# The attention stage of an RWKV-type block on eight cores: the order of its k, v and r projections, and where the Sigmoid stands

## What is computed

```python
xn = _ln(x, ln1_g, ln1_b)
xp = _shift(xn)
k = (xn * mix_k + xp * (1.0 - mix_k)) @ Wk
v = (xn * mix_v + xp * (1.0 - mix_v)) @ Wv
r = jax.nn.sigmoid((xn * mix_r + xp * (1.0 - mix_r)) @ Wr)
# wkv: a = ew * a + exp(k_t) * v_t;  b = ew * b + exp(k_t);  out = a / (b + 1e-8)
wkv = _wkv(k, v, time_decay, time_first)
x = x + r * wkv @ Wo
yn = _ln(x, ln2_g, ln2_b)          # ... then channel mixing and the FFN
```

## Time and profile before

| | |
|---|---|
| Time, median of 3 runs (lowest to highest) | 4658.79 us (4657.66 to 4661.13) |
| Profiled execution: its time, span of core 5 | 4664.68 us, 4663.1 us |
| Spans of the eight cores | 4631.3 to 4663.1 us |
| PE, PEld busy | 3025.4 us (65%), 1208.8 us (26%) |
| DVE busy | 1479.8 us (32%) |
| ACT busy | 1278.9 us (27%) |
| Table loads at line 650 and at line 656 | 64 and 64, 1283 ns each |
| Chain that ended last, by engine | PE 39%, DMA 20%, DVE 20%, ACT 11%, issue 8% |

### The profile page before, as it was taken

How to read it: one execution, slowest core, us unless ns; L and a number is a source line. 1 busy time by engine, 2 the same in 40 slices (tenths; PEclk the granted TensorE clock), 3 DMA queues, 4 the chain that set the end, 5 groups by cost and what they waited for, 6 DMA issues and landing times.

```text
span 4663.1 us, 41167 instructions; the slowest of 8 cores (4631.3 to 4663.1 us)
## 1 busy us (share of the span) xinstructions
PE 3025.4 (65%) x11840; PEld 1208.8 (26%) x11840; DVE 1479.8 (32%) x2843; ACT 1278.9 (27%) x1846; POOL 168.6 (4%) x292
## 2 busy tenths in 40 slices
PE   1112289968468856876486847695587558775867
PEld 0000023223123312332132313331233223321322
DVE  3212323421452144214422253214511552135221
ACT  1132232221421323221432242224313242214221
POOL 2111201200000000000000000000000000000000
PEclk9556566679679977988798968897898779896988
DMA  7565446534223321433132412342243214340323
GB/s 152 159 190 167 150 153 192 178 99 124 71 79 118 111 90 61 129 102 125 52 113 85 130 72 90 88 131 88 75 122 105 97 52 127 99 138 36 115 90 111
DMA packets 260844, 521.09 MB, mean 112 GB/s; under 512 B 26081, under 2 KB 81633, under 8 KB 250386
## 3 DMA queue, kind: packets, MB, share of 16 engines
q1 hardware_dynamic: 178096, 387.52, 26.6%
q0 software_dynamic: 24192, 79.28, 5.3%
q10 hardware_dynamic: 58338, 51.66, 3.9%
HBM read 457.54 MB, written 60.82 MB: 111 GB/s over the span
## 4 chain that ended last, share of the span: by engine, by line
PE 39%; DMA 20%; DVE 20%; ACT 11%; issue 8%; DVEq 1%; POOL 1%; ACTq 1%; SPq 0%; POOLq 0%
PE psO L809 14%; PE psA L841 9%; PE psB L841 8%; DMA fvb<-s_w 3%; DMA fvb<-s_fv 3%; DMA s_w<-stb 2%; DVE bigbf L580 2%; DVE stB_sum L497 2%; DVE sc_bb L571 2%; DMA s_fv<-stb 2%; DVE sc_bb L663 2%; ACT L650 2%; ACT L656 2%; DVE sc_aa L701 1%; PE psT L544 1%
## 5 line engine op out<-in xcount | busy, mean ns | idle before, releaser
L809 PE MATMUL psO<-fvb,bigbf 128*128 128x512 bf16 x4096 | 1078.5, 399 | 217.0 <-DMA fvb<-s_w 68.1
L613 PE MATMUL psO<-bigbf,wsm 128*128 128x512 bf16 x1024 | 341.9, 491 | 531.5 <-ACT bigbf L650 220.8
L809 PEld LDWEIGHTS psO<-fvb,bigbf 128*128 128x128 bf16 x4096 | 393.5, 101 | 841.8 <-issue 461.4
L841 PE MATMUL psB<-TB,fkb 128*128 128x512 bf16 x2048 | 522.4, 401 | 41.1 <-DMA fkb<-s_fk 36.3
L841 PE MATMUL psA<-TB,fkb 128*128 128x512 bf16 x2048 | 514.8, 397 | 21.0 <-DMA fkb<-s_fk 13.4
L867 DVE TENSOR_TENSOR bigbf<-bigbf 128x512 bf16<-128x512 bf16 x256 | 108.4, 425 | 688.0 <-ACT bigbf L863 688.0
L934 DVE SCALAR_TENSOR_TENSOR T<-Q,psO 128x512 f32<-128x512 f32 x64 | 44.0, 688 | 860.4 <-PE psO L927 855.0
L613 PEld LDWEIGHTS psO<-bigbf,wsm 128*128 128x128 bf16 x1024 | 113.7, 116 | 754.0 <-issue 694.9
L506 ACT ACTIVATE zt<-T,stB_nm 128x1024 bf16<-128x1024 f32 x64 | 73.5, 1148 | 851.7 <-DVE stB_m L503 849.2
L841 PEld LDWEIGHTS psB<-TB,fkb 128*128 128x128 bf16 x2048 | 206.7, 102 | 325.5 <-issue 125.1
L544 PE MATMUL psT<-ident_sb,ztm 128*128 128x128 bf16 x512 | 69.6, 292 | 332.6 <-DVE ztm L523 194.4
(11 more groups left out here) (138 smaller groups left out, 3094.5 us busy)
## 6 DMA issues: line engine op xcount, KB each, us to landing
fkb<-s_fk SPq DMA_DIRECT2D x256, 256.0 KB, 2.8
fvb<-s_fv SPq DMA_DIRECT2D x256, 256.0 KB, 2.8
fkb<-s_w SPq DMA_DIRECT2D x256, 256.0 KB, 2.8
fvb<-s_w SPq DMA_DIRECT2D x256, 256.0 KB, 2.8
stq<-L_ffn_fc_q ACTq DMA_DIRECT2D x128, 256.0 KB, 4.4
x<-xcore SPq DMA_DIRECT2D x8, 2048.0 KB, 10.1
wsm<-s_wk SPq DMA_DIRECT2D x16, 1024.0 KB, 7.0
wsm<-s_wr SPq DMA_DIRECT2D x16, 1024.0 KB, 8.9
```

Of the source, the lines that this page charges most:

```text
L613: E("tensor", lambda e, mo=mo, k=k, ps=ps, wt=wt: e.matmul(ps[:], wt[:, 1024 * (k % 4) + 128 * mo:1024 * (k % 4) + 128 * (mo + 1)], bigbf[ ...
L809: E("tensor", lambda e, mm=mm, j=j, mpar=mpar, sl=sl: e.matmul(psO[j][:], bigbf[:, 512 * mm + 128 * j:512 * mm + 128 * (j + 1)], fvb[:, 10 ...
L841: E("tensor", lambda e, m=m, k=k, ps=ps, par=par: e.matmul(ps[:], fkb[:, 1024 * par + 128 * k:1024 * par + 128 * (k + 1)], TB[:, 512 * k:5 ...
```

## The change

The v loop and the scan for b become one loop, and the r loop moves behind it.

- After the k loop comes a loop over `mo` with the v projection and, on VectorE in this order, `ekv`, `sa`, `ca`, `sb`, `cb`, `wk`; on ScalarE `ew`, `lb`, `eb`. One decay tile serves both scans, and `ew2` is gone. `eb` writes back into `sc_bb`, and `wk` multiplies `sc_aa` with it into `T2`.
- A last loop has the r projection. Sigmoid goes into a new tile `rsg` (128 x 512, one buffer) and `gt` multiplies it with `T2`. Sigmoid and `gt` of block `mo` are recorded behind the matmuls of block `mo` + 1.
- The weight buffers hold other matrices: Wv's halves are in `wsm2` and `wsm0`, Wr's in `wsm1` and `wsm2`, Wo's in `wsm0` and `wsm1`.
- In chunk 0 the cast jobs come in the order Wk, Wv, Wr, and of the 52 pairs 10 stand ahead of `stage_mix_vr`, 24 in the k loop, 8 in the v loop (both casts on ScalarE), and the last 10 in the first five passes of the r loop. None is left for the Wo loop.

The diff, without the removed v loop (old lines 687 to 721), the call that records the last Sigmoid, and the two added `pump_pair()` calls ahead of chunk 0:

```diff
@@ -234,6 +234,7 @@
+        rsg = T("rsg", [128, 512], BF16)
@@ -357,8 +358,8 @@
-        for wname, whbm, scr in [("s_wk", Wk, s_wk), ("s_wr", Wr, s_wr),
-                                 ("s_wv", Wv, s_wv), ("s_wo", Wo, s_wo),
+        for wname, whbm, scr in [("s_wk", Wk, s_wk), ("s_wv", Wv, s_wv),
+                                 ("s_wr", Wr, s_wr), ("s_wo", Wo, s_wo),
                                  ("s_wfr", Wfr, s_wfr)]:
@@ -624,8 +625,8 @@
-            E("q_sync", lambda e: e.dma_start(out=wsm[2][:], in_=s_wr[0]),
-              reads=["s_wr@0", "s_wr@1"], writes=["wsm2"], tag=f"{hh}_ldr0")
+            E("q_sync", lambda e: e.dma_start(out=wsm[2][:], in_=s_wv[0]),
+              reads=["s_wv@0", "s_wv@1"], writes=["wsm2"], tag=f"{hh}_ldv0")
@@ -640,17 +641,18 @@
                     pump_pair()
                     pump_pair()
-            E("q_sync", lambda e: e.dma_start(out=wsm[0][:], in_=s_wr[1]),
-              reads=["s_wr@0", "s_wr@1"], writes=["wsm0"], tag=f"{hh}_ldr1")
-            E("q_sync", lambda e: e.dma_start(out=wsm[1][:], in_=s_wv[0]),
-              reads=["s_wv@0", "s_wv@1"], writes=["wsm1"], tag=f"{hh}_ldv0")
+                    pump_pair()
+            E("q_sync", lambda e: e.dma_start(out=wsm[0][:], in_=s_wv[1]),
+              reads=["s_wv@0", "s_wv@1"], writes=["wsm0"], tag=f"{hh}_ldv1")
+            E("q_sync", lambda e: e.dma_start(out=wsm[1][:], in_=s_wr[0]),
+              reads=["s_wr@0", "s_wr@1"], writes=["wsm1"], tag=f"{hh}_ldr0")
             for mo in range(KT):
-                ps, psn = kvr_mm(hh, mo, wsm[2], "wsm2", wsm[0], "wsm0", 16,
-                                 f"{hh}_rmm", pool=RPS)
-                E("scalar", lambda e, mo=mo, ps=ps: e.activation(
-                    out=bigbf[:, 512 * (24 + mo):512 * (25 + mo)], in_=ps[:],
-                    func=AF.Sigmoid),
-                  reads=[psn], writes=[bbuf(24 + mo)], tag=f"{hh}_sg{mo}")
+                ps, psn = kvr_mm(hh, mo, wsm[2], "wsm2", wsm[0], "wsm0", 8,
+                                 f"{hh}_vmm")
+                E("vector", lambda e, mo=mo, ps=ps: e.tensor_tensor(
+                    out=sc_ekv[:], in0=T1[:, 512 * mo:512 * (mo + 1)], in1=ps[:],
+                    op=OP.mult),
+                  reads=["T1", psn], writes=["ekv"], tag=f"{hh}_ekv{mo}")
                 sl_e = mo % 2
                 ese = slice(512 * sl_e, 512 * (sl_e + 1))
@@ -658,6 +660,15 @@
+                E("vector", lambda e, mo=mo, ese=ese: e.tensor_tensor_scan(
+                    out=sc_aa[:], data0=ew_t[:, ese],
+                    data1=sc_ekv[:], initial=vca[:, mo:mo + 1],
+                    op0=OP.mult, op1=OP.add),
+                  reads=[f"ewt{sl_e}", "ekv"], sreads=["vca"], writes=["aa"],
+                  tag=f"{hh}_sa{mo}")
+                E("vector", lambda e, mo=mo: e.tensor_copy(
+                    out=vca[:, mo:mo + 1], in_=sc_aa[:, 511:512]),
+                  sreads=["aa"], writes=["vca"], tag=f"{hh}_ca{mo}")
@@ -673,52 +684,42 @@
-                E("scalar", lambda e, mo=mo, bo=bo: e.activation(
-                    out=T2[:, 512 * mo:512 * (mo + 1)],
-                    in_=sc_bb[:, bo:bo + 512], func=AF.Exp, scale=-1.0),
-                  sreads=[bn], writes=["T2"], tag=f"{hh}_eb{mo}")
+                E("scalar", lambda e, bo=bo: e.activation(
+                    out=sc_bb[:, bo:bo + 512], in_=sc_bb[:, bo:bo + 512],
+                    func=AF.Exp, scale=-1.0),
+                  sreads=[bn], writes=[bn], tag=f"{hh}_eb{mo}")
+                E("vector", lambda e, mo=mo, bo=bo: e.tensor_tensor(
+                    out=T2[:, 512 * mo:512 * (mo + 1)], in0=sc_aa[:],
+                    in1=sc_bb[:, bo:bo + 512], op=OP.mult),
+                  reads=["aa", bn], writes=["T2"], tag=f"{hh}_wk{mo}")
+                if h == 0:
+                    pump_pair("scalar", "scalar")
+            E("q_sync", lambda e: e.dma_start(out=wsm[2][:], in_=s_wr[1]),
+              reads=["s_wr@0", "s_wr@1"], writes=["wsm2"], tag=f"{hh}_ldr1")
+            E("q_sync", lambda e: e.dma_start(out=wsm[0][:], in_=s_wo[0]),
+              reads=["s_wo@0", "s_wo@1"], writes=["wsm0"], tag=f"{hh}_ldo0")
+            sig_fns = []
+            for mo in range(KT):
+                ps, psn = kvr_mm(hh, mo, wsm[1], "wsm1", wsm[2], "wsm2", 16,
+                                 f"{hh}_rmm", pool=RPS)
+                def mkf(mo=mo, ps=ps, psn=psn):
+                    E("scalar", lambda e: e.activation(
+                        out=rsg[:], in_=ps[:], func=AF.Sigmoid),
+                      reads=[psn], writes=["rsg"], tag=f"{hh}_sg{mo}")
+                    E("vector", lambda e: e.tensor_tensor(
+                        out=bigbf[:, 512 * (24 + mo):512 * (25 + mo)],
+                        in0=rsg[:], in1=T2[:, 512 * mo:512 * (mo + 1)],
+                        op=OP.mult),
+                      reads=["rsg", "T2"], writes=[bbuf(24 + mo)],
+                      tag=f"{hh}_gt{mo}")
+                sig_fns.append(mkf)
+                if mo > 0:
+                    sig_fns[mo - 1]()
                 if h == 0:
                     pump_pair()
                     pump_pair()
```

More of the change, by code:

```diff
@@ L682, in stage_attn @@
                     pump_pair()
-            E("q_sync", lambda e: e.dma_start(out=wsm[2][:], in_=s_wv[1]),
-              reads=["s_wv@0", "s_wv@1"], writes=["wsm2"], tag=f"{hh}_ldv1")
-            E("q_sync", lambda e: e.dma_start(out=wsm[0][:], in_=s_wo[0]),
-              reads=["s_wo@0", "s_wo@1"], writes=["wsm0"], tag=f"{hh}_ldo0")
-            for mo in range(KT):
-                ps, psn = kvr_mm(hh, mo, wsm[1], "wsm1", wsm[2], "wsm2", 8,
-                                 f"{hh}_vmm")
-                E("vector", lambda e, mo=mo, ps=ps: e.tensor_tensor(
-                    out=sc_ekv[:], in0=T1[:, 512 * mo:512 * (mo + 1)], in1=ps[:],
-                    op=OP.mult),
-                  reads=["T1", psn], writes=["ekv"], tag=f"{hh}_ekv{mo}")
-                sl_e = mo % 2
-                ese = slice(512 * sl_e, 512 * (sl_e + 1))
-                E("scalar", lambda e, mo=mo, ese=ese: e.activation(
-                    out=ew_t[:, ese], in_=ew_t[:, ese], func=AF.Exp, scale=0.0,
-                    bias=vtd[:, mo:mo + 1]),
-                  reads=[f"ewt{sl_e}"], sreads=["vtd"], writes=[f"ewt{sl_e}"],
-                  tag=f"{hh}_ew2{mo}")
-                E("vector", lambda e, mo=mo, ese=ese: e.tensor_tensor_scan(
-                    out=sc_aa[:], data0=ew_t[:, ese],
-                    data1=sc_ekv[:], initial=vca[:, mo:mo + 1],
-                    op0=OP.mult, op1=OP.add),
-                  reads=[f"ewt{sl_e}", "ekv"], sreads=["vca"], writes=["aa"],
-                  tag=f"{hh}_sa{mo}")
-                E("vector", lambda e, mo=mo: e.tensor_copy(
-                    out=vca[:, mo:mo + 1], in_=sc_aa[:, 511:512]),
-                  sreads=["aa"], writes=["vca"], tag=f"{hh}_ca{mo}")
-                E("vector", lambda e, mo=mo: e.tensor_tensor(
-                    out=T2[:, 512 * mo:512 * (mo + 1)], in0=sc_aa[:],
-                    in1=T2[:, 512 * mo:512 * (mo + 1)], op=OP.mult),
-                  reads=["aa", "T2"], writes=["T2"], tag=f"{hh}_wk{mo}")
-                E("vector", lambda e, mo=mo: e.tensor_tensor(
-                    out=bigbf[:, 512 * (24 + mo):512 * (25 + mo)],
-                    in0=bigbf[:, 512 * (24 + mo):512 * (25 + mo)],
-                    in1=T2[:, 512 * mo:512 * (mo + 1)], op=OP.mult),
-                  reads=[bbuf(24 + mo), "T2"], writes=[bbuf(24 + mo)],
-                  tag=f"{hh}_gt{mo}")
-                if h == 0:
-                    pump_pair("scalar", "scalar")
@@ L722, in stage_attn @@
+            sig_fns[KT - 1]()
             E("q_sync", lambda e: e.dma_start(out=wsm[1][:], in_=s_wo[1]),
```

## The result

The changed kernel took 4549.96 us (median of 9 runs, 4537.3 to 4673.8) against 4662.77 for the kernel before in the same comparison (10 runs, 4657.66 to 4869.84). In some executions the cores of one die ran some per cent slower than the others, whatever the kernel: these are in the medians and ranges, and left out of every ratio. The ratio is **0.9757, 95% interval 0.9745 to 0.9769**. The profiled execution took 4549.96 us; the trace read here is that of its slowest core, core 1, with a span of 4548.4.

The account below looks back on a forecast made before the run. ScalarE, VectorE and TensorE were taken to work in turns, chained through the r loop with its table loads. 4664.7 - 146 (later chunks) + 12 (chunk 0) = 4530.7, less 5.9 for the median: 4525 us, range 4492 to 4580.

Parts of the forecast that it names:

- Pass of the merged loop: Merged v loop and scan for b: 6.11 us from start to start, no table load, decay tile hidden.
- The new wait for Wo: Wo projection: TensorE waits 2 to 5 us for Wo's second half, loaded into `wsm1` after the last r block.
- the bound where TensorE is slow throughout: Later chunks: r blocks take 20.2 us, last 8 matmuls 3.3, first add at 77, net gain 12.8 us.
- Ln's added table load: Layer norm: its Ln now follows a Sigmoid and needs a table load on the path, 1.28 us a chunk.
- Net gain of a later chunk: Chunks 1 to 7: 22.2 us gained up to the first add, less the table load, net 20.9 each.
- Chunk 0: First chunk, attention stage set by cast jobs: loses about 12 us, between 20 gained and 40 lost.
- two pairs more ahead of the mixing: Chunk 0 casts: 17 us less for the rest, against about 3 delaying the mixing, so 14 us saved.
- no pair saved: Chunk 0 lower bound: the 12 or so Wfk pairs, forecast to save 9 us, save nothing.
- chain not hidden: Chunk 0 lower bound: merged loop's 5.4 us chain between pairs not hidden by load and write waits; forecast +1, range 0 to +8.
- Rival 1: r loop: TensorE runs at 0.42 us a matmul throughout, gain 90 less 12, total 4581 us; chance 8%.
- Rival 2: Chunk 0: Wfv pairs wait for the merged loop's full chain, 38 us more, total 4563; chance 8%.
- Rivals 3 and 4: Merged loop: two table loads stay in each pass, 4674 us, chance 4%; or passes take 10.83 us, 4790, chance 1%.

Follow-up runs that it names:

- casts_old: Changed kernel with chunk 0's cast pairs handed out as in the kernel before (two fewer ahead of the mixing, 16 in the k loop); ratio to before 0.9711.
- wk_late: Changed kernel with each pass's `wk` recorded behind the scans of the next pass, `sc_aa` in two halves; ratio to the kernel before 0.9685.

## Why the prediction was right, step by step

Right in its cause, and within 25 us in its size: 4525 forecast, 4550 measured, inside the range. Against the profiled execution's own time the change was to bring 134 us and brought 4664.7 - 4550.0 = 114.7. The 5.9 us that the forecast took off for the median did not come either: here the profiled execution is the median. The other 19.3 lie in the later chunks (3), in chunk 0 (8) and in the slowest core (7); 1 stays unassigned.

- **Pass of the merged loop: 6.11 forecast, 6.02 measured.** No load in it. One pass in chunk 7 took 6.37; the mean over cores and chunks is 6.04.
- **Start of the r loop.** On core 1 the first Sigmoid came at 4165.65 - 4116.34 = 49.3, forecast 49.5.
- **The r projection: 12.5 us forecast, 12.83 for 48 matmuls.** TensorE's timeline, with the Wo projection behind it:

```profile
4166.39 12.83 PE L614 MATMUL psO<-bigbf,wsm 128*128 128x512 bf16 x48 [21.80 <-ACT rsg L707]
...
4180.56 0.38 PE L740 MATMUL psO<-wsm,bigbf 128*128 128x512 bf16 x1
4185.56 0.59 PE L734 MATMUL psO<-wsm,bigbf 128*128 128x512 bf16 x1 [4.62 <-DMA wsm<-s_wo]
4185.94 0.63 PE L740 MATMUL psO<-wsm,bigbf 128*128 128x512 bf16 x1
4186.37 0.63 PE L734 MATMUL psO<-wsm,bigbf 128*128 128x512 bf16 x1
```

- **The new wait for Wo: right in place and in size.** Forecast 2 to 5 us in every chunk; over all eight of core 1 it is 23.7 us, 3.0 on average, and 4.62 in the chunk shown, where the load landed some 2 us later than forecast. From the view of line 723 in the changed kernel:

```profile
  PE psO L734: 23.7, 8
...
DMA to landing us min/median/max: 4.8/4.9/6.9
```

- **What I had not seen in it:** behind the wait the matmuls stand 0.43 us apart instead of 0.216 and are back at 0.22 some 6 us later. The granted clock was 0.50 from 4185.56 to 4191.40, TensorE's lower level of 1.2 GHz. In chunk 7 of core 1 the 8 matmuls up to the first add took 3.2 us instead of the 1.8 forecast, and the add stands at T + 72.5; the mean over cores and chunks is 69.26 against 68.6 forecast. It is not this chunk alone: in chunks 1 to 7 of the six cores with complete records these 8 matmuls took 2.5 us on average, behind idle times of 2.6 us in the median, and only in 7 of 42 did they keep 0.22 throughout. That is the 0.7 by which the add came late. The prediction has 3.3 us for them only in the bound where TensorE is slow throughout; in its sum they stand at full pace right behind the wait that it had itself named.
- **Ln's added table load: 1.28 forecast, 1.18 by the means (39.42 - 38.24).** The timeline of ScalarE shows it in full on the path:

```profile
4210.23 1.28 ACT L517 ACT_TABLE_LOAD   x1
4211.52 0.30 ACT L517 ACTIVATE stB_rs<-stB_vs,ce 128x4 f32<-128x4 f32 x1
```

  The Ln starts 1.29 us behind the start of its load, without the drain of 1.38 that the Trainium skill (ScalarE: Activation LUTs, "What ACT_TABLE_LOAD costs") adds to every switch. None shows ahead of a load either: in the earlier trace rows one starts at 4230.54, 0.02 us behind the end of the Sigmoid.
- **Net gain of a later chunk: 20.9 forecast, 20.4 measured.** Times 7: 146 against 143. A part of this agreement is luck. From mixing to add the forecast was 22.2 and the means give 20.8: 0.7 less because one chunk of one core (90.77) stood for the mean of 90.08, 0.7 for the matmuls behind the wait for Wo. The 0.8 in stages that the change leaves alone make up for half of it. A slip in the bounds changed nothing: 90.8 - 77 - 1.28 is 12.5, not 12.8.
- **Chunk 0: the mis-sized term.** Forecast a loss of 12, measured 19.6 at the first rr (mean of the cores), inside its bounds of 20 gained to 40 lost. Of its parts, "two pairs more ahead of the mixing" failed: I let them cost the mixing 3 us, the work of their casts, and they cost it 162.2 - 146.3 = 15.9, nearly the 17 they save later. A pair costs about 8 us wherever it stands, it seems; what holds it up ahead of the mixing wasn't tested by itself, but casts_old, with two pairs fewer there, has the mixing end at 144.7. On core 1 the last cast starts at 556.2 instead of the 547 forecast, where it was at 568.7 before. By the means over the cores it is 548.6 after 565.9, so 17.3 earlier where 21.7 were forecast. That the total is so near is luck too, since the two pairs brought 13 us less than forecast and the other terms some 8 more: the 24th of the 104 casts comes only 2.9 us earlier than before on average, the 66th 20.3 and the 88th 4.7. Why the lead comes and goes like this stays open. The last cast stands in the fifth pass of the r loop, as forecast, and the uncovered tail has the forecast shape:

```profile
556.23 1.06 ACT L344 ACTIVATE stb<-stf 128x1024 bf16<-128x1024 f32 x1 [13.20 <-DMA stf<-L_attn_Wfv]
557.19 0.58 ACT L707 ACTIVATE rsg<-psO 128x512 bf16<-128x512 f32 x1
...
592.66 1.28 ACT L517 ACT_TABLE_LOAD   x1
593.96 0.30 ACT L517 ACTIVATE stB_rs<-stB_vs,ce 128x4 f32<-128x4 f32 x1
```

  From last cast to Ln are 37.7 us against 35 forecast (37.4 by the means). So the 12 forecast became 19 at the Ln: 4.4 from the later last cast, 2.4 from the longer tail. casts_old shows that this tail is what costs: with casts left to cover it, 16.5 of the 19.6 come back. By its own terms (no pair saved 9, chain not hidden 7) the lower bound would be 28 lost and not 40; the loss lay inside that too.
- **The slowest core.** By the means the sum is -143 + 20 = -123, and the mean span fell by 122.0. The time is that of the slowest core, which stands 23 us above the mean in this profile and stood 16 above it before. These 7 us are the rest of the difference, and they are within the scatter: over nine executions of each kernel the slowest core stood 13 to 30 us above the mean before and 15 to 25 after. The prediction took one core's rows for the time; why one core falls behind wasn't tested.

Rival 1 (cold TensorE in the r loop) didn't occur as put; a short form of it sits behind the wait for Wo. Rival 2 (the merged loop's chain in full in chunk 0) didn't: 19.6 lost, not 50. Rivals 3 and 4 are ruled out by the pass of 6.02 us with no load in it. The decay tile's time was hidden in the merged loop, as the prediction said, but only because `wk` waited there (wk_late).
